# Moving one group's causal mask of a fused attention kernel from TensorE matmuls to a VectorE add in PSUM

## The reference

```
x = x + 0.5 * moe(layernorm(x))
x = x + attn(layernorm(x))          # attn(y) = y + softmax(mask + (y Wq / 8)(y Wk)^T) (y Wv) Wo
x = x + 0.5 * moe(layernorm(x))
```

## Time and profile before

| | |
|---|---|
| median of 3 runs | 1430.07 us (1429.7 to 1431.35) |
| the profiled execution, its own time | 1428.43 us |
| its span | 1426.7 us |
| busy: TensorE matmul, weight load | 1393.1 us (98%), 981.4 us (69%) |
| busy: VectorE, ScalarE, GpSimd | 1165.5 us (82%), 855.6 us (60%), 438.4 us (31%) |
| TensorE clock granted | full speed in nearly all of the span |
| DMA in the attention | 1 to 2 GB/s |

### The profile page before, as it was taken

One profiled execution on the slowest core, in us unless ns is written; L12 is line 12 of the kernel. 1 busy time (PEld: TensorE's weight loads), 2 busy tenths in 40 slices (PEclk: granted clock), 3 DMA queues, 4 the chain that ended last, 5 costly groups with the idle time before them and its releaser, 6 DMA issues.

```text
span 1426.7 us, 27934 instructions
## 1 busy us (share of the span) xinstructions
PE 1393.1 (98%) x9781; PEld 981.4 (69%) x9781; DVE 1165.5 (82%) x2520; ACT 855.6 (60%) x2011; POOL 438.4 (31%) x688
## 2 busy tenths in 40 slices
PE   5999999999999999999999999999999999999998
PEld 4667677767766667676767776776667677767775
DVE  8888988898778777777777778778878888888885
ACT  4355445444467788787878777877645344534542
POOL 1022112201334444444434444443422112202220
PEclk9999999999999999999999999999999999999999
DMA  6443333333310000000000000000033433344332
GB/s 239 147 137 106 118 107 114 114 107 118 113 38 2 2 2 2 2 2 2 2 2 2 2 2 2 2 2 1 2 124 102 121 120 121 107 121 126 115 117 91
DMA packets 59171, 98.22 MB, mean 69 GB/s; under 512 B 6176, under 2 KB 15648, under 8 KB 59040
## 3 DMA queue, kind: packets, MB, share of 16 engines
q1 hardware_dynamic: 59040, 96.51, 21.5%
HBM read 92.82 MB, written 3.67 MB: 68 GB/s over the span
## 4 chain that ended last, share of the span: by engine, by line
PE 85%; DVE 8%; ACT 2%; issue 2%; POOL 1%; DMA 1%; SPq 0%; DVEq 0%; ACTq 0%
PE banks L204 16%; PE banks L206 14%; PE banks L205 14%; PE banks L455 12%; PE banks L595 10%; PE banks L560 9%; PE banks L581 6%; PE banks L570 2%; PE banks L405 2%; DVE work L1232 1%; PE banks L417 1%; DVE nmax L1355 1%; DVE work L1241 1%; ACT work L911 1%; DVE stage L1370 1%
## 5 line engine op out<-in xcount | busy, mean ns | idle before, releaser
L810 ACT ACTIVATE work<-banks 128x512 f32<-128x512 f32 x320 | 189.3, 596 | 354.1 <-PE banks L206 344.5
L1241 DVE TENSOR_TENSOR work<-banks,work 128x512 f32<-128x512 f32 x320 | 220.3, 689 | 89.7 <-ACT work L810 86.6
L911 ACT ACTIVATE work<-banks,nmax 128x512 f32<-128x512 f32 (+3 forms) x512 | 263.9, 526 | 41.4 <-DVE nmax L1355 36.1
L1232 DVE TENSOR_TENSOR work<-work 128x512 f32<-128x512 f32 x320 | 258.1, 807 | 6.4 <-DMA work<-cw_rows 2.0
L1531 POOL TENSOR_SCALAR work<-work,rrec 128x512 f32<-128x512 f32 (+3 forms) x512 | 262.7, 535 | 0.0
L455 PE MATMUL banks<-work,wd 128*128 128x512 f32 x460 | 234.9, 594 | 0.5 <-DVE work L1232 0.2
L204 PE MATMUL banks<-xT_hi,wg_hi 128*128 128x512 f32 x336 | 222.4, 662 | 0.4 <-DVE wu_lo L1223 0.4
L1355 DVE TENSOR_REDUCE nmax<-banks 128x2 f32<-128x1024 f32 (+3 forms) x256 | 195.5, 806 | 3.2 <-PE banks L570 3.2
L1507 POOL TENSOR_TENSOR k_hi<-work,q_hi 128x512 fp32r<-128x512 f32 x51 | 75.3, 1482 | 301.4 <-ACT q_hi L814 301.1
L1370 DVE COPY stage<-banks 128x1024 f32<-128x1024 f32 (+1 forms) x128 | 122.0, 953 | 38.5 <-PE banks L581 38.1
L1507 POOL TENSOR_TENSOR k_lo<-work,q_lo 128x512 fp32r<-128x512 f32 x50 | 73.5, 1475 | 234.2 <-ACT q_lo L814 233.8
(11 more groups left out here) (159 smaller groups left out, 2662.9 us busy)
## 6 DMA issues: line engine op xcount, KB each, us to landing
work<-cw_rows SPq DMA_DIRECT2D x320, 256.0 KB, 3.2
x<-in_x SPq DMA_DIRECT2D x8, 256.0 KB, 6.9
out_rows<-x SPq DMA_DIRECT2D x8, 256.0 KB, 2.2
cw_rows<-cwT SPq DMA_DIRECT2D x16, 96.0 KB, 2.0
stage<-in_w_gate SPq DMA_DIRECT2D x3, 448.0 KB, 5.0
stage<-in_w_up SPq DMA_DIRECT2D x2, 448.0 KB, 6.3
wd<-in_w_down SPq DMA_DIRECT2D x2, 448.0 KB, 6.9
stage<-in_wq SPq DMA_DIRECT2D x1, 512.0 KB, 3.8
```

The source lines that it names most:

```text
L810: nc.scalar.activation(silu[j % 2], psG[j % 3], ACT.Silu).then_inc(s["silu_done"], 1)
L911: m = nc.scalar.activation(prob[:, p % 2, i, o:o + w], ps[:, i, so:so + w], ACT.Exp, bias=nmax[:, p % 2, i, qb:qb + 1], accum_out=rsum[:, ...
L1232: tt(z[part_slot(j)], gated[j % 3], spread[:, j % NSPREAD, :], ALU.mult) \
L1241: tt(gated[j % 3], psU[j % 3], silu[j % 2], ALU.mult).then_inc(s["gated_done"], 1)
```

## The change

The mask of group u = 0 alone is added by VectorE: TensorE's four mask matmuls of that group go, VectorE gets one `tensor_tensor` add of 128 x 2 x 128 elements (f32 in PSUM, in place, plus a 128 x 128 bf16 mask broadcast over the two heads), before the maximum of the group, and the maximum waits for it by a new semaphore. Groups 1 and 2 stay as they were. The constant grows by 128 columns, and one small routing tile now lies inside another to make room.

```diff
@@ constants
-    small = np.concatenate([ident, iota, tie.reshape(P, -1), *halves], 1)
+    small = np.concatenate([ident, iota, tie.reshape(P, -1), *halves, mask], 1)
@@ build
-        half = sb("half", [P, 6 * P], BF16)
+        half = sb("half", [P, 7 * P], BF16)
+        mask = half[:, 6 * P:]
...
-        half_f32 = work[:, 5 * CH:5 * CH + 6 * P]
+        half_f32 = work[:, 5 * CH:5 * CH + 7 * P]
...
-            [sb("gcmp_2", [P, TB, G, G])[:, :, :, :]]
+            [gcmp_2]
@@ TensorE, scores
-                            pe.matmul(ps[:, i, o:o + w], qk[0][a][r, p % 2, qb * P:(qb + 1) * P],
-                                      qk[1][c][r, p % 2, 0:w], start=qb != 0 and k == 0, stop=False,
-                                      skip_group_check=True)
+                            m = pe.matmul(ps[:, i, o:o + w], qk[0][a][r, p % 2, qb * P:(qb + 1) * P],
+                                      qk[1][c][r, p % 2, 0:w], start=qb != 0 and k == 0,
+                                      stop=u == 0 and k == 2, skip_group_check=True)
+                if u == 0:
+                    m.then_inc(s["s_ps"], 1)
+                    return
@@ VectorE
+            def mask_scores(b, p):
+                n = pair(b, p)
+                dve.wait_ge(s["s_ps"], 3 * n + 1)
+                ps = score_banks(p, 0)[:, :, 3 * P:]
+                tt(ps, ps, mask[:, :].unsqueeze(1).broadcast_to([P, 2, P]), ALU.add).then_inc(s["masked"], 1)
+
             def row_max(b, p, u):
                 n = pair(b, p)
-                dve.wait_ge(s["s_ps"], 3 * n + u + 1)
+                if u == 0:
+                    dve.wait_ge(s["masked"], n + 1)
+                else:
+                    dve.wait_ge(s["s_ps"], 3 * n + u + 1)
@@ VectorE, attn_slot
                 if have_s:
+                    mask_scores(*ahead(b, p, 1))
                     row_max(*ahead(b, p, 1), 0)
                     row_max(*ahead(b, p, 1), 1)
@@ VectorE, attention
+                mask_scores(0, 0)
                 row_max(0, 0, 0)
```

More of the change, by code:

```diff
@@ L143, in build @@
         gscore = sb("gscore", [P, TB * G, 1])
+        onehot = sb("onehot", [P, TB, E, TOPK])
+        gcmp_2 = onehot[:, :, :, :].rearrange("p t e k -> p (t e k)")[:, 0:TB * G * G] \
+            .rearrange("p (t a b) -> p t a b", t=TB, a=G)
         gcmp = [t[:, :, :].rearrange("p (t a) b -> p t a b", t=TB) for t in t4] + \
-            [sb("gcmp_2", [P, TB, G, G])[:, :, :, :]]
+            [gcmp_2]
         grank, gpen = t1[0], t1[1]
@@ L150, in build @@
         topf = sb("topf", [P, TB, 8])
-        onehot = sb("onehot", [P, TB, E, TOPK])
         wts = masked
@@ L183, in build @@
             a_xn a_xT_ps a_xT_hi a_xT_lo a_xres
-            q_ps k_ps v_ps q_hi q_lo k_hi k_lo v_sb s_ps max_done exp_done rec_done norm_done
+            q_ps k_ps v_ps q_hi q_lo k_hi k_lo v_sb s_ps masked max_done exp_done rec_done norm_done
             pT_ps pT_act pT_dve ctx_ps ctx_hi ctx_lo out_ps outT_sb outT_ps out_added stored""".split()
```

## The result

The change makes the kernel slower. The median goes from 1430.51 us (1429.7 to 1431.35, 4 runs) to 1450.94 us (1450.41 to 1453.05, 4 runs), a ratio of 1.0148 on record with a 95% interval of 1.0135 to 1.0161 (the quotient of the two medians is 1.0143): about 20 us more, where 14.1 were forecast. The mechanism is the forecast one, two of its terms were too small, and the result lies at the upper edge of the range (1451), by the ratio just beyond it (1.0148 x 1430.07 = 1451.2).

What follows compares the result with a forecast made beforehand. Bound: a loop TensorE, VectorE, ScalarE, VectorE, TensorE with 0.20 us slack, nearly as long as TensorE's own work. 12.3 - 0.5 + 1.0 + 1.35 = 14.1 us on 1428.43 gives 1442.5; medians stood 1.6 higher: 1444.2 us, range 1437 to 1451.

Steps and rivals of the forecast that it cites:

- sign (e): Trace of the attention: slots p = 4 would not get longer.
- 49 ordinary slots: Mid-attention slots: the loop would need 9.71 us instead of 9.46, +0.25 each, 12.3 us in all.
- seven slots p = 4: Slots with an extra ScalarE operation before the exponentials: delay covered, some TensorE gain comes through, -0.05 us each.
- the two other covered slots: Slots in the last two sequences with the next feed-forward's preparation: delay covered, -0.05 us each.
- the end: Last slots, without projections to hide behind: three full delays of the maximum, +1.35 us.
- the start: Pipeline filling at the start of attention: the first mask add and the second delay everything, +1.0 us.
- rival 3: The add in PSUM costs as 512 elements: delay 0.71 us, +0.51 per ordinary slot, 1459 us; 13% for over 1450.
- the delay of the maximum's start: VectorE, group 0: add of 0.417 us plus 0.03 semaphore wait makes the maximum start 0.45 us later.
- The delay is covered: Slots p = 4: exponentials wait for an extra ScalarE operation, not the maximum, so the slots gain 0.05 us each.
- 1 (the gain arrives): TensorE stays the bound and its shorter stream counts: all of it would be 11 us, 1419 us; 5%.
- 2 (a draw): Delay near 0.20 to 0.25 us, say because ScalarE catches up somewhere: 1428 to 1432 us; 4%.
- 4 (k_lo): TensorE waits for k_lo before group 2's last mask matmuls: +0.1 us per slot, 1449 us; no chance given.

Runs made afterwards that it cites:

- experiments 1: Changed kernel, but TensorE keeps its four mask matmuls of the widest group, so it is masked twice: 1451.05 us against 1429.25 for the kernel before.
- experiment 3: Kernel before with three or eight tiny VectorE copies ahead of the widest group's maximum: 1429.94 us (three) and 1448.14 us (eight) against 1430.68.
- experiment 2: Changed kernel without VectorE's add and its wait, the widest group left unmasked: 1420.97 us against 1429.25 for the kernel before.
- `start_before`: Changed kernel with the mask of the first three pairs left on TensorE: 1449.42 us against 1429.13 for the kernel before.
- Experiment 5: Changed kernel with xT_lo put ahead of the maximum of group 1 in slots p = 4: 1447.37 us against 1429.13 for the kernel before.

## Why the prediction was wrong in size

The direction, the mechanism and most of what would be seen in the trace held (sign (e), slots p = 4 not longer, did not): a loop through four hand-overs with a slack of 0.20 us (experiments 1 and 3), TensorE's saving of 0.18 real but off the path (2), `attend` waiting for q_lo and starting 0.05 behind it. The sum was 14.1 us and the median moved by 20.4. Term by term, from the distances between the 64 `attend`s of the first profiles, and for start and end from profiles of the same code without a fall of the clock there (the end from that of `start_before`, which is the changed kernel there):

| term of the sum | forecast | measured |
|---|---|---|
| 49 ordinary slots | +12.3 | +15.0 |
| seven slots p = 4 (six x 0.29, and 0.58) | -0.35 | +2.3 |
| the two other covered slots | -0.1 | -0.35 |
| the end (last five distances) | +1.35 | +1.6 |
| the start | +1.0 | +0.8 |
| sum | 14.1 | 19.4 |

The prediction rounded the nine covered slots to -0.5, hence 14.1. Of the 20.4 us of the medians 1.0 is left over. The falls of the clock, of which the profiles have from none to three between 400 us and the last ten, are one source that large: the kernel before takes 392.15 us behind its last `attend` in one profile and 393.75, with one fall, in the other. The larger constant and the moved tile show no cost: the first product of the scores starts at 413.15 and 413.60 in the changed kernel's profiles and at 412.70 and 413.45 before, and behind the last `attend` the changed kernel takes 392.17 and 393.74.

- **The delay was mis-sized.** The add itself was well priced: 0.407 us by its mean, 0.417 forecast, and no dearer for its destination in PSUM, so rival 3 fell. The Trainium skill's 62 cycles more for touching PSUM ("VectorE: DVE Perf Modes", section "The TRN2 errata"), charged a second time for the destination, would have made it an estimated 0.48: the trace disagrees. The hand-off was right too. What failed was the step that took the delay of the maximum's start, 0.45, for the delay of the loop: the loop goes by its end, and its row grew from 1.175 to 1.226. The trace of the kernel before had one such row, the first maximum at 414.58 with 1.23, and the prediction did not use it. With 0.30 per slot the ordinary slots give 14.7; two that stand next to small VectorE work give the rest.
- **"The delay is covered" in slots p = 4 was wrong.** The step looked at who else holds the exponentials, and found cover. It didn't ask who waits for the work queued behind the maxima: xT_lo (L1334 of the kernel before), and TensorE's projection behind it. The list of what is queued behind the add named both maxima, k_lo and q_lo, and left out this one, which is there in one slot of eight. Experiment 5 shows that this was the main fault: without that wait six of the seven come out at 9.77, 0.02 below before, where -0.05 was forecast. The seventh, the first in time, stays 0.25 above before: there VectorE's layernorm work comes on top, and ScalarE waits 0.38 us for the maximum.
- **The start** was about right: 0.8 by the clock of the profile, 1.1 counted from the first scores, 1.0 forecast. The first pair of profiles seemed to say 3.2, because the clock fell in one and not in the other.
- **Rivals.** 1 (the gain arrives) is what experiment 2 looks like, and 2 (a draw) is what experiment 3's short delay looks like; the real delay is two and a half times the slack. 4 (k_lo) happened in part: TensorE does wait about 0.25 us for k_lo in every ordinary slot. But what follows up to `attend` takes 0.70 (experiment 2), so that wait alone would end the slot at 9.53, and q_lo, which the rival had some 0.2 later, ends it at 9.76.

## What to carry to other kernels

An engine that is busy all the time need not be the only bound: walk back from one of its instructions through what each waits for, and see whether the walk comes back to the same engine one round earlier; the slack of that loop is the price limit for anything put into it. The same operation, on the same engine, was free in ordinary slots in front of an instruction that waits for others, and cost 0.30 us in each in front of one that others wait for. And when something is delayed, go through every variant of the loop body for what is queued behind it, since the rare slot has the instruction that the usual one lacks.

## What the runs showed of the hardware

- Four short matmuls in front of a larger one cost more than themselves: about 0.09 us from their start to the next, and as much again as the first product behind them took 0.26 to the next start and not 0.17. In the trace the weight load of that next product starts 0.08 behind the first product then, and together with it without the mask. Removing them gave 0.18 per slot (experiment 2: 9.28 against 9.46).
- An add on VectorE that reads and writes PSUM in place, 256 elements, took 0.407 us, no more than the reduction of the same size out of PSUM (0.417).
- The maximum over 1024 elements (two heads of 512) took 1.175 us right behind a reciprocal, 1.23 wherever it had waited for the add or for TensorE, in the kernel before too, and 1.22 behind a row of tiny copies. The cause is open.
- TensorE's granted clock fell to half in one execution and not in another at the same place of the same program. Two falls at the start of the attention went with a first `attend` 2 us later in the kernel before (437.18 and 439.14).
- A busy share can hide waits: in the changed slot TensorE's idle times come to 0.23 us, the distances of starts show 0.48 lost.
